# Stationaries of two heads for q, k and mix, with longer unread products and another order of loads in the front, in an attention and FFN kernel

## The reference

```python
# D = 64 rows, L = 512 columns, 8 heads of Lh = 64 columns
def attention(xq, xk, xv):
    q, k, v = Wq @ xq + bq, Wk @ xk + bk, Wv @ xv + bv      # for each batch
    scores = einsum('hbdk,hbek->hbde', q_h, k_h) / sqrt(Lh)
    p = softmax(scores, axis=-1)
    return Wo @ einsum('hbde,hbek->hbdk', p, v_h) + bo
def ffn(x):                                                  # H = 512, I = 1792
    gate, up = silu(x @ dequantize(gate_w)), x @ dequantize(up_w)
    return (gate * up) @ dequantize(down_w)
x = x + attention(layernorm(x), ctx, ctx)
x = x + ffn(layernorm(x))
```

## Time and profile before

| what | us |
|---|---|
| time, median of 3 runs | 437.23 (437.18 to 437.42) |
| the profiled execution's own time | 437.11 |
| its span, first to last instruction | 435.3 |
| TensorE busy | 412.4 (95%) |
| TensorE's weight loads | 318.4 (73%) |
| ScalarE busy | 331.0 (76%) |
| VectorE busy | 329.2 (76%) |
| GpSimd busy | 265.7 (61%) |

### The profile page before, as it was taken

One profiled execution on the slowest core, in us unless ns is written; L12 is line 12 of the kernel. 1 busy time (PEld: TensorE's weight loads), 2 busy tenths in 40 slices (PEclk: granted clock), 3 DMA queues, 4 the chain that ended last, 5 costly groups with the idle time before them and its releaser, 6 DMA issues.

```text
span 435.3 us, 10739 instructions
## 1 busy us (share of the span) xinstructions
PE 412.4 (95%) x4220; PEld 318.4 (73%) x4220; DVE 329.2 (76%) x582; ACT 331.0 (76%) x540; POOL 265.7 (61%) x265
## 2 busy tenths in 40 slices
PE   7978988998989999999999999999999999999994
PEld 4745666776756778677777878677877888888872
DVE  3778666998878876787887877877887666667676
ACT  2257898897876788686878878687878998988970
POOL 3345787899588555755564855754576555555561
PEclk9999999999998999999999999999999999999998
DMA  7678845876842001001011001000010000001003
GB/s 247 193 231 246 290 146 202 294 220 205 232 135 73 2 2 26 5 22 45 32 50 26 0 2 26 26 2 26 14 39 0 2 1 0 26 24 48 2 1 96
DMA packets 26792, 35.44 MB, mean 81 GB/s; under 512 B 1870, under 2 KB 18422, under 8 KB 26742
## 3 DMA queue, kind: packets, MB, share of 16 engines
q1 hardware_dynamic: 26434, 34.71, 24.7%
q10 hardware_dynamic: 244, 0.05, 0.1%
q0 software_dynamic: 64, 0.00, 0.0%
HBM read 30.56 MB, written 4.19 MB: 80 GB/s over the span
## 4 chain that ended last, share of the span: by engine, by line
PE 70%; DVE 9%; issue 8%; POOL 6%; ACT 5%; DMA 1%; SPq 1%; POOLq 0%; DVEq 0%; ACTq 0%
PE banks L766 19%; PE banks L768 18%; PE banks L779 10%; PE banks L780 9%; PE banks L665 3%; DVE yT L1039 3%; PE banks L705 2%; PE banks L694 2%; ACT banks L557 2%; PE banks L675 2%; PE banks L683 2%; POOL t_sb L418 1%; DMA x_sb<-in_x 1%; DVE st L923 1%; POOL wgu_in L411 1%
## 5 line engine op out<-in xcount | busy, mean ns | idle before, releaser
L557 ACT ACTIVATE banks<-banks,ratio 128x512 f32<-128x512 f32 x336 | 208.1, 663 | 35.5 <-PE banks L768 25.9
L1039 DVE SCALAR_TENSOR_TENSOR yT<-banks,sd,yT 128x512 f32<-128x512 f32 x208 | 154.2, 747 | 49.2 <-PE banks L780 48.3
L766 PE MATMUL banks<-xT,wgu 128*128 128x512 f32 x448 | 182.6, 408 | 4.6 <-DVE t_sb L1024 2.5
L768 PE MATMUL banks<-xT,wgu 128*128 128x512 f32 x448 | 175.5, 392 | 0.0
L418 POOL TENSOR_TENSOR t_sb<-t_sb,u_sb 128x512 f32<-128x512 f32 x56 | 72.8, 1299 | 63.3 <-DVE t_sb L1024 63.2
L766 PEld LDWEIGHTS banks<-xT,wgu 128*128 128x128 f32 x448 | 84.4, 188 | 26.5 <-issue 3.7
L768 PEld LDWEIGHTS banks<-xT,wgu 128*128 128x128 f32 x448 | 84.5, 189 | 15.3
L779 PE MATMUL banks<-hr,wd 128*128 128x512 f32 x224 | 89.6, 400 | 4.9 <-DVE yT L1039 3.0
L780 PE MATMUL banks<-hr,wd 128*128 128x512 f32 x224 | 87.7, 392 | 0.0
L431 POOL TENSOR_TENSOR hr<-t_sb,hr 128x512 fp32r<-128x512 f32 x56 | 73.1, 1305 | 5.1 <-ACT hr L579 0.7
L779 PEld LDWEIGHTS banks<-hr,wd 128*128 128x128 f32 x224 | 42.2, 188 | 20.0 <-DVE yT L1039 10.3
(11 more groups left out here) (94 smaller groups left out, 383.6 us busy)
## 6 DMA issues: line engine op xcount, KB each, us to landing
x_sb<-in_x SPq DMA_DIRECT2D x16, 256.0 KB, 6.1
out<-x_sb SPq DMA_DIRECT2D x16, 256.0 KB, 2.2
wgu_in<-in_L_ffn_gate_w SPq DMA_DIRECT2D x7, 512.0 KB, 6.2
z_in<-in_L_ffn_gate_z SPq DMA_DIRECT2D x7, 512.0 KB, 5.5
wgu_in<-in_L_ffn_up_w SPq DMA_DIRECT2D x7, 512.0 KB, 6.2
z_in<-in_L_ffn_up_z SPq DMA_DIRECT2D x7, 512.0 KB, 4.9
wd_in<-in_L_ffn_down_w SPq DMA_DIRECT2D x7, 512.0 KB, 5.5
z_in<-in_L_ffn_down_z SPq DMA_DIRECT2D x7, 512.0 KB, 4.8
```

What stands on the lines that cost most here:

```text
L557: act.activation(banks[:, bank, :], banks[:, bank, :], ACT.Copy, scale=ratio[:, m, g, it:it + 1]).then_inc(done[n % 2], 1)
L766: pe.matmul(banks[:, bank, :], w, xT[:, c % 2, 0, g, :], start=g == 0, stop=False, skip_group_check=True)
L768: pe.matmul(banks[:, bank, :], w, xT[:, c % 2, 1, g, :], start=False, stop=True, skip_group_check=True).then_inc(full[n % 2], 1)
L1039: dve.scalar_tensor_tensor(y, bank, sd[:, it, b:b + 1], y, ALU.mult, ALU.add).then_inc(s_free, 1)
```

## The change

In `project` and `mix` the two heads that wrote the two halves of the output's partitions become one stationary of 64 rows and 128 columns, with the same moving operand. The number of matmuls falls from 32 to 16 in project and from 16 to 8 in mix. For mix the two heads have to lie side by side in `e_sb`, so `score` writes its pairs of heads to other columns (`to`); its matmuls stay as they are. In the front three unread products get longer (2 to 3, 1 to 3 and 3 to 5 blocks of 128 columns), and SP loads x 2 ahead of context 1.

```diff
             sync.dma_start(wraw[:, 1, :], Wk).then_inc(s_wsm, 16)
-            for t in range(2):
-                load_x(t)
-                load_ctx(t)
+            load_x(0)
+            load_ctx(0)
+            load_x(1)
             load_x(2)
+            load_ctx(1)
             load_x(3)
...
                 for m, src in enumerate((xn[:, t % 2, :], ctx_of(t))):
                     for c in range(NC):
-                        for b, hp in TURNS:
-                            r, k = HALVES[b], HALVES[hp]
-                            h = 2 * c + hp
-                            mm = pe.matmul(banks[k, at + b, (m * NC + c) * D:(m * NC + c + 1) * D],
-                                           src[r, h * Lh:(h + 1) * Lh], wT[r, m, :], start=True, stop=True)
+                        for b, r in enumerate(HALVES):
+                            mm = pe.matmul(banks[:, at + b, (m * NC + c) * D:(m * NC + c + 1) * D],
+                                           src[r, 2 * c * Lh:2 * (c + 1) * Lh], wT[r, m, :], start=True, stop=True)
...
-                        mm = pe.matmul(banks[o, at + hp, c * D:(c + 1) * D], qkT[r, b, c * D:(c + 1) * D],
+
+                        to = 2 * (c % 2) + c // 2
+                        mm = pe.matmul(banks[o, at + hp, to * D:(to + 1) * D], qkT[r, b, c * D:(c + 1) * D],
                                        qkT[r, b, (NC + c) * D:(NC + c + 1) * D], start=True, stop=True)
...
                 for j in range(NC):
-                    for b, g in TURNS:
-                        r, o = HALVES[b], HALVES[g]
-                        h = NC * g + j
-                        mm = pe.matmul(banks[o, 6 + b, j * D:(j + 1) * D], e_sb[r, t % 2, h % 2, h // 2, :], wT[r, 3, :],
-                                       start=True, stop=True)
+                    for b, r in enumerate(HALVES):
+
+                        mm = pe.matmul(banks[:, 6 + b, j * D:(j + 1) * D], e_sb[r, t % 2, j % 2, 2 * (j // 2):2 * (j // 2) + 2, :].rearrange("p g e -> p (g e)"),
+                                       wT[r, 3, :], start=True, stop=True)
...
-            stir(2)
+            stir(3)
             pe.wait_ge(s_wT, 1)
             project(0)
...
-            stir(1)
+            stir(3)
             score(0)
             project(1)
...
-            stir(3)
+            stir(5)
             pe.wait_ge(s_sub, 1)
             score(1)
```

## The result

The changed kernel takes 455.74 us (454.39 to 456.84, 4 runs), the kernel before 437.33 us beside it; the ratio is 1.041, 95% interval 1.037 to 1.045. The forecast was 457.4 us. The profiled execution of the changed kernel took 456.84 us, the longest of its four, with a span of 455.0 us.

The account below looks back on a forecast made before the run. TensorE was taken as the bound behind the front. Main loop 12.9 us plus front 7.4 us made 20.3 us on the profiled execution's 437.1 us, giving 457.4 us, range 444 to 472 us.

Parts of the forecast that it names:

- The pitch of a round: Project and mix bursts: the load of 128 columns sets each round, 112 ns against 58, so 0.053 us more.
- Project's +0.85 us: Each project burst at full clock: 16 rounds, each 0.053 us longer, add 0.85 us.
- mix's +0.43 us: Each mix burst at full clock: 8 rounds, each 0.053 us longer, add 0.43 us.
- The change of shape: Bursts of apply and mix: switching from 64x64 to 64x128 costs between 0 and 0.27 us, 0.15 taken.
- The main loop: From 45.9 to 325 us: longer projects, mixes and changes of shape, less idle time recovered, add 12.9 us.
- given back: Main loop: TensorE's idle time absorbs part of the added burst time, 2.5 us up to 150 us, 0.5 us after.
- The front: Before the main loop: score(1) 4.2 us late, then 3.2 us more from project(2) on, 7.4 us in all.
- Behind the last burst: The stretch from 325 us on, without attention work: nothing changes.
- Rival D: A with the clock low for longer because the array multiplies half the time: 461 to 470 us, chance 0.16.
- A: Project and mix: the load of 128 columns sets the round; 449 to 463 us, likeliest 457.4 us, chance 0.64.
- B: Project and mix: a wide load costs no more than two narrow ones; 434 to 436 or 438 to 440 us, chance 0.13.
- C: Project and mix: the halves of the rows load one after the other, 219 ns a round; about 497 us, chance 0.07.

## Why the prediction was right

**The pitch of a round.** The step that carried the sum held: 0.110 us for seven steps, where I had 0.112, from rows of 128x128 loads only. That the load and not the multiplication is the reason is shown by the doubled columns. The Trainium skill (TensorE: Matmul & The Clock Gate, LDWEIGHTS) has the load go by columns and not by rows; this case's loads of 64 rows by 128 columns agree, 188 ns like those of 128 rows:

```profile
L664 PEld LDWEIGHTS banks<-wT,ctx_sb x192: 188/188/228, 49.3 to 306.7; 64*128 64x128 f32 x192
...
L664 PEld LDWEIGHTS banks<-wT,ctx_pre x64: 188/259/330, 9.1 to 31.0; 64*128 64x128 f32 x64
```

Project's +0.85 us was +0.84; mix's +0.43 us was +0.58 with the change of shape, of which I had 0.43 + 0.15.

**The change of shape** is real between 64x64 and 64x128: 0.20 us from load to load against 0.03, and the first wide load no longer lies under apply's last round. I took the middle of the bounds. From 0.58 - 0.43 it is 0.15 us a burst. That the middle of the bounds was exact is luck: no row pointed at it.

**The main loop.** Forecast +12.9 us, in the two profiles +12.8. The bursts added 15.7 us (I had 15.9), so 2.9 us were given back (I had 3.0). Whether they were given back for my reason, engines that catch up during a burst, is not shown. Against 273.1 us both forms together took 15.2 us more, which would leave 0.5 us given back; against the 275.2 us of the kernel before, whose profile has a dip at 132 to 136 us, it is 2.6 us. And the dips can't be priced from the table: the stretch takes 288.0 us in the changed kernel, which has one at 61 to 64 us, and 288.3 and 287.5 us in two kernels with the same rounds and none.

**The front.** score(1) was to be 4.2 us late and is 4.4. All the steps of this part are seen: the first product is hidden, project(0)'s additional time is half covered, and x 2's earlier landing is worth nothing, since VectorE has been waiting 2.38 us when project(0) ends. (x 2 is taken up at 7.64 us instead of 9.40, so it came at least 1.8 us earlier and not 0.7.) From score(1) to the first FFN matmul I had +3.2 us and it is +1.7: the 2.01 us without a reason have gone with the instructions, and I had taken 2 us off for this and everything else. This term is mis-sized by 1.5 us. And the 52.0 us at which the front ends belong to this execution: with the same instructions it ended at 56.4 us in another. That the front's 7.4 us came so near to 6.0 is partly luck: the two kernels that have this front took from 454.4 to 460.7 us.

**Behind the last burst** I had nothing, and it is +0.9 us in this execution, through a dip at 447 to 450 us. In the executions of most other kernels here this stretch is as long as before.

**What I priced too low.** My sum counts the front's wide loads at half speed only up to score(1), and in the profiled execution that holds: full speed comes within project(2), as in the kernel before it comes right behind project(2). Rival D had a mechanism that is real (with wide stationaries the clock stays low for longer), and I gave it 0.16. The other profiles with wide, unfilled projects are at half speed up to 29.4, 31.6 and 33.9 us (past 36 us in the run of 465.13 us), the four with narrow ones up to 13.2, 13.4, 13.6 and 19.8 us, and the five with filled ones up to 11.2 us at most. The one comparison with a single edit, the filling, moves the end of the front from 54.0 to 45.8 us with the same loads. The stationaries alone, at 461 us, lie at the lower end of D's range. The changed kernel's four runs of 454.4 to 456.8 us lie in A's; why its profiled execution reached full speed at 23.2 us is not shown.

The dip at 61 to 64 us is not explained either. It stands behind a wait of 1.1 us and a project of two heads, and the FFN matmuls last 0.63 us instead of 0.40 for 3 us:

```profile
61.31 0.79 PE L766 MATMUL banks<-xT,wgu 128*128 128x512 f32 x1
...
64.46 0.40 PE L768 MATMUL banks<-xT,wgu 128*128 128x512 f32 x1
```

The stationaries alone have the same wait of 1.1 us ahead of the same project, and no dip.

**The ranges.** The bounds that the prediction lists for A (5.8 us down and 7.5 us up from 457.4) give 451.6 to 464.9 us, not to the 449 to 463 us that it states; the forecast itself and the outcome are not touched by it.

**The rivals that fell.** B wanted a round under 60 ns: 110. The exception for FP32 that the prediction names agrees with the 188 ns for 128 columns above. C wanted 3 us and more for a project: 1.93. Loads in the two halves of the rows run side by side, also with 128 columns.

## What to carry to other kernels

Stationaries that are as wide as possible halve the instructions, not the time. With little to multiply behind each, the pitch goes by the columns of one load (0.110 us for 128, 0.058 us for 64), and four quarters that load 64 columns at once are nearly twice as fast as two halves that load 128. Read the pitch from start to start, once for the loads and once for the matmuls, before merging small matmuls. If the array is idle under a load and the clock is at its lower level, columns multiplied twice cost nothing here and brought full speed much earlier (9.8 us instead of 31.6); once it is there, go back to the form with the shorter round.

## What was not expected of the hardware

**Instructions arrive in blocks, and a block can be late.** TensorE's instruction queue moved 33 packets before and 27 after, 0.54 and 0.44 MB: 16 KB each, and one packet less for each 255 of the 1532 instructions that are gone. (33 times 256 is 8448, where 8440 loads and matmuls are shown, and 27 times 256 is 6912, where it is 6908.) In the front a stretch without work comes at the same count of matmuls whatever stands there. TensorE's count up to that stretch, in the kernel before, with only the front's edits, and with only mix (start:end, length, busy and number of each engine; the PEld or PE number is the one to read):

```profile
0.00:24.80 24.80, 21.49 (x470) 15.50 (x474) 14.54 (x39) 7.31 (x12) 7.72 (x17) 1.00 0.74 238
```

```profile
0.00:23.60 23.60, 20.78 (x474) 1.00 0.76 237
```

```profile
0.00:25.60 25.60, 21.89 (x473) 1.00 0.73 233
```

474, 474 and 473 matmuls, at 25.3, 23.9 and 25.7 us, once behind `values`, once within it, once within `mix`; the stretch is 2.0, 2.6 and 1.5 us long. The kernel before with doubled columns has it at 474 matmuls too, 4.5 us long. With four wide, filled projects it comes at 346 matmuls, 0.8 us long: 128 matmuls and as many loads fewer, 256 instructions. The weights' pieces, 512 KB each, are under way then. That the fetch waits behind them is argued from this and was not tried by itself. The changed kernel has fewer instructions and shows no such stretch over 0.7 us in its front. A long stretch can cost more than itself: behind those of 2.6, 1.5, 4.5 and 2.9 us (the last with tile 0 filled) the granted clock is 0.50 for 3 to 7 us, behind that of 2.0 us in the kernel before it is not.

**The clock's rise in the front is not the same in each execution.** With the same instructions up to score(0), full speed came at 19.8 us in the kernel before and at 13.4 us in the one with only mix changed. What decided between them no run here shows. With wide stationaries the spread is larger (23.2 and 33.9 us with the same instructions). This is most of why single profiles of the front disagree, and why the sum of the parts can't be checked there to better than a few microseconds.
